# Two attention layers on one core: a per-batch schedule, looped over the batches, replaced by one written-out list over all sixteen units

## The reference, cut to what matters

```python
# layer 0                                     # layer 1
q, k, v = split(xn @ Wqkv.T)                  kc = conv(xn, Wconv, stride=3); k_tmp = cat(xn[:, :1], kc)
scores = q @ k.T / sqrt(8)                    q = xn @ Wq.T; k = k_tmp @ Wk.T; v = k_tmp @ Wv.T
scores = where(qi >= ki, scores, -inf)        scores = q @ k.T / sqrt(8) - 1e9 * (3*ki >= qi + 0.001)
o = softmax(scores) @ v; x += o @ Wo.T        o = softmax(scores) @ v; x += o @ Wo.T + bo
```

## Time and profile before

| | |
|---|---|
| median of 3 runs | 1368.36 us (1366.69 to 1369.11) |
| profiled execution | 1375.63 us, its span 1373.7 us |
| attention of layer 0 | 246.8 to 766.9 us of the span |
| attention of layer 1 | 886.1 to 1124.9 us |
| mean granted clock of TensorE | 0.903 of full |

### The profile page before, as it was taken

The page is one execution under the profiler, slowest core; times in us unless marked ns, Lnnn a source line. Parts: engine busy times, 40 slices in busy tenths (PEclk is TensorE's granted clock), DMA queues, the critical chain, the costliest instruction groups (busy, mean ns, idle before and its releaser), DMA issues. The chain is left out here.

```text
span 1373.7 us, 25353 instructions
## 1 busy us (share of the span) xinstructions
PE 1147.1 (84%) x7394; PEld 634.9 (46%) x7394; DVE 1012.1 (74%) x2140; ACT 721.2 (52%) x1105; POOL 562.2 (41%) x821
## 2 busy tenths in 40 slices
PE   0665667899989998999999666699999969999984
PEld 0433455334434443444343344444444427888863
DVE  5997999788868886888784254477767627777788
ACT  0552222056656665666567442045656557777772
POOL 5455322013423331333222253346667571565663
PEclk9877898599999999999999787579999889999996
DMA  3333790001221211121100023112222115577542
GB/s 100 93 117 112 115 109 0 3 15 60 89 88 48 71 63 57 48 71 63 40 2 2 1 75 99 40 33 65 57 56 68 33 56 186 168 234 237 178 123 62
DMA packets 98595, 107.75 MB, mean 78 GB/s; under 512 B 16226, under 2 KB 76455, under 8 KB 98481
## 3 DMA queue, kind: packets, MB, share of 16 engines
q1 hardware_dynamic: 93488, 97.83, 26.1%
q0 software_dynamic: 4992, 8.48, 1.8%
HBM read 64.67 MB, written 42.63 MB: 78 GB/s over the span
## 5 line engine op out<-in xcount | busy, mean ns | idle before, releaser
L1105 ACT ACTIVATE a_probs<-a_pst 128x1024 f32<-128x1024 f32 (+4 forms) x544 | 417.9, 812 | 276.5 <-PE a_pst L1035 274.1
L1130 DVE TENSOR_REDUCE a_tops<-a_ps 128x1 f32<-128x512 f32 (+9 forms) x624 | 343.4, 589 | 77.4 <-PE a_ps L1004 73.0
L946 POOL TENSOR_SCALAR_AFFINE_SELECT a_probs<-a_probs 128x256 f32<-128x256 f32 (+3 forms) x384 | 181.7, 482 | 429.5 <-ACT a_probs L1105 426.3
L1004 PE MATMUL a_ps<-kp,qp 96*128 96x512 bf16 (+9 forms) x1280 | 313.4, 314 | 8.6 <-issue 6.6
L1035 PE MATMUL a_pst<-qp,kp 99*128 99x512 bf16 (+4 forms) x1088 | 264.4, 336 | 5.4 <-ACT a_probs L1105 4.6
L1058 PE MATMUL a_po<-a_probs,vh 128*32 128x512 f32 (+4 forms) x2176 | 233.6, 501 | 7.5 <-POOL a_probs L946 6.7
L1130 DVE TENSOR_REDUCE a_tops_lead<-a_ps 128x1 f32<-128x512 f32 x256 | 166.9, 685 | 39.4 <-PE a_ps L1004 36.9
L1004 PEld LDWEIGHTS a_ps<-kp,qp 96*128 96x128 bf16 x1280 | 115.0, 103 | 118.1 <-DVE a_tops_lead L1130 34.0
L1001 PE MATMUL a_ps<-mask_s,identb 128*128 128x128 bf16 (+8 forms) x624 | 148.5, 239 | 12.7 <-DVE a_tops L1130 4.7
L1035 PEld LDWEIGHTS a_pst<-qp,kp 99*128 99x128 bf16 (+1 forms) x1088 | 97.7, 101 | 79.1 <-ACT a_probs L1105 36.9
L1001 PEld LDWEIGHTS a_ps<-mask_s,identb 128*128 128x128 bf16 x624 | 60.1, 99 | 153.8 <-DVE a_tops L1130 90.3
(11 more groups left out here) (262 smaller groups left out, 1800.6 us busy)
## 6 DMA issues: line engine op xcount, KB each, us to landing
e_slot_w<-weight_parts SPq DMA_DIRECT2D x23, 1024.0 KB
weight_parts<-a_cut SPq DMA_DIRECT2D x18, 512.0 KB, 4.2
k_parts<-o SPq DMA_DIRECT2D x48, 128.0 KB
qp<-q_parts SPq DMA_DIRECT2D x64, 96.0 KB
kp<-k_parts SPq DMA_DIRECT2D x32, 192.0 KB
slot_rows<-empty_row SPq DMA_DIRECT2D x4, 1495.0 KB, 26.8
e_slot_x<-slot_rows SPq DMA_DIRECT2D x23, 260.0 KB, 3.6
a_raw<-in_wraw SPq DMA_DIRECT2D x18, 256.0 KB, 4.3
```

The lines of the kernel that those rows point to most:

```text
L946: pool.affine_select(out=seen, in_=seen, compare_op=ALU.is_ge, fill=0.0, base=m0, pattern=[[0, 2], [1, mw]], channel_multiplier=-1 if laye ...
L1004: last = pe.matmul(bank[:, i * room:i * room + w], sb["qp"][slot][0:KROWS, j, f["qt"] * P:(f["qt"] + 1) * P], sb["kp"][slot][0:KROWS, j // ...
L1105: act.activation(probs[local % RING][0:st["rows"], 2 * part:2 * part + 2, st["off"]:CHUNK], p_st[part][0:st["rows"], :, st["off"]:CHUNK], ...
L1130: dve.tensor_reduce(out, scores, AX.X, ALU.max).then_inc(s["banks_read"], 1)
```

## The change

`batch_schedule`, `TUNING`, `batches` and the hardware loop go. `Geometry.order` makes one list for all sixteen units of a layer. It steps through time: it keeps a clock for each of PE, DVE, ACT and POOL, gives each operation a duration from constants at the top of the file, and appends at each step the entry whose inputs are ready first (with a rank where several are ready). The engines' code then has batch and unit numbers that are constants, in both layers. The arithmetic, the tiles, the number of banks (3) and of buffers for probabilities (4) are as before.

```diff
-TUNING = [(13, 2800, 2200), (13, 2500, 2200)]
+COLUMN_US, LOAD_US, PASS_US, LANE_US, REDUCE_US, EXP_US, EXP_COLUMN_US, TAIL_US, STORE_US, LOADED_US = (
+    0.00042, 0.105, 0.07, 0.00104, 0.165, 0.17, 0.00083, 1.1, 2.2, 9.0)
+AHEAD = (0.35, 0.6)
+RING = 4
...
+            if n < units and (k or n in maxima_end) and (n * S + k < RING or n * S + k - RING in sums_end):
+                ready.append((max(pe, score_banks[half] + PASS_US, maxima_end[n]), 3, "pair"))
...
+            m, f = fills // F, fills % F
+            if m < units and m in loaded and m < n + 2 and not (turns and f == F - 1) and (m < 2 or m - 2 in split_end):
+                behind = m + fills_share[f] < at + 1 + AHEAD[self.layer]
+                ready.append((max(bank, loaded[m]), 2 if behind else 5, "fill"))
+            start, _, what = min((r if r[0] > pe + PASS_US else (pe, r[1], r[2])) for r in ready)
...
+            if what == "turn_max":
+                m = turns.pop(0)
+                pe = start + LOAD_US
+                banks[mine] = dve = max(dve, pe + PASS_US) + REDUCE_US
+                maxima_end[m] = dve + STORE_US
+                order.append(("turn_max", m, 0, 0))
...
+                if k == S - 1 and half and n + GROUPS < units:
+                    order.append(("next_load", n, 0, 0))
+                    loaded[n + GROUPS] = pe + LOADED_US
...
-        def batches(eng, body):
-
-            if layer == 0:
-                with eng.Fori(0, B - 1) as b:
-                    body(b, geo.batch_schedule(False, False), False)
-            else:
-                for b in range(B - 1):
-                    body(b, geo.batch_schedule(False, False), False)
-            body(B - 1, geo.batch_schedule(False, True), True)
...
+            for what, n, k, part in order:
...
+                if what == "turn_max":
+                    sp.wait_ge(s["banks_read"], read(use))
+
+                    sp.dma_start(sb["qp"][n % GROUPS][KROWS:KROWS + PARTS, :, :].rearrange("r j t -> r (j t)"),
+                                 top_rows[:, :]).then_inc(s["maxima_stored"], 16)
+                if what == "next_load":
+                    sp.wait_ge(s["scores_t_ready"], since["scores_t_ready"] + 2 * S * (n + 1))
+                    load_operands(sp, sb, dram, layer, geo.keys, n // GROUPS + 1, n % GROUPS)
```

More of the change, by code:

```diff
@@ L713, in __init__ @@
         self.split = 5 if layer == 0 else 4
[L717 to L799, removed]
@@ L806, in counted_before @@
     ends = T // CHUNK * units
-    uses = geo.uses_before(B - 1, False) + geo.last_uses
+    uses = sum(what in BANK_USES for what, *_ in geo.order())
     layer0 = dict(banks_filled=uses, banks_read=uses, split_steps=units * geo.split, maxima_stored=16 * units, scores_t_ready=2 * units * geo.S,
@@ L844, in attention, with filled, read @@
         block = ctx.enter_context(nc.Block())
[L846 to L852, removed]
+        order = geo.order()
+        def filled(use):
+            return since["banks_filled"] + use + 1
+        def read(use):
+            return since["banks_read"] + use + 1
         def raw_load(sp, b, i):
             sp.wait_ge(e["cut_done"], START + 2 * (BATCH_CUTS * b + max(0, i - 1)))
-            sp.dma_start(raw[i % 2][:, :], io["wraw"][bass.ds(b * BATCH_CUTS + i, 1), :, :].rearrange("c p h -> (c p) h"))\
+            sp.dma_start(raw[i % 2][:, :], io["wraw"][b * BATCH_CUTS + i, :, :])\
                 .then_inc(sb["raw_in"][i % 2], 16)
@@ L1056, in weigh @@
                 for j in range(GH):
-                    last = pe.matmul(p_o[VW * j:VW * (j + 1), c0:c1], sb["vh"][g % 2][0:st["rows"], st["kt"], j, :],
-                                     probs[local % RING][0:st["rows"], j, c0:c1],
-                                     start=st["first"] and half == 0, stop=st["last"], tile_position=(0, VW * j),
+                    last = pe.matmul(p_o[VW * j:VW * (j + 1), st["off"]:CHUNK], sb["vh"][n % 2][0:st["rows"], st["kt"], j, :],
+                                     probs[local % RING][0:st["rows"], j, st["off"]:CHUNK],
+                                     start=st["first"], stop=st["last"], tile_position=(0, VW * j),
@@ L1061, in weigh @@
                                      skip_group_check=True)
-                if half == len(halves) - 1:
-                    last.then_inc(s["pv_done"], 1)
-            def run(b, schedule, last):
-                use = 0
-                for what, g, k, part in schedule:
-                    if what == "fill":
-                        fill(b, g, k, use)
-                    if what == "pair":
-                        pair(b, g, k, part, g * S + k)
-                    if what == "weigh":
-                        weigh(b, g, k, part, g * S + k)
-                    if what == "turn_max":
-                        turn_max(b, b * GROUPS + g, use)
-                    if what == "turn_out":
-                        turn_out(b, b * GROUPS + g, k, use)
-                    use += what in BANK_USES
@@ L1080, in first @@
-            def first(schedule):
-                for use, (what, g, k, part) in enumerate(x for x in schedule if x[0] in BANK_USES):
-                    if what == "fill":
-                        fill(0, g, k, use, first=True)
-                    if what == "turn_max":
-                        turn_max(0, 0, use, first=True)
-            first(geo.batch_schedule(True, False))
-            batches(pe, run)
+                last.then_inc(s["pv_done"], 1)
+            use = 0
+            for what, n, k, part in order:
+                if what == "fill":
+                    fill(n, k, use)
+                if what == "pair":
+                    pair(n, k, part)
+                if what == "weigh":
+                    weigh(n, k)
+                if what == "turn_max":
+                    turn_max(n, use)
+                if what == "turn_out":
+                    turn_out(n, k, use)
+                use += what in BANK_USES
@@ L1115, in _ @@
-            batches(act, run)
+            use, last_out = 0, None
+            for what, n, k, part in order:
+                if what == "turn_out":
+                    last_out = use
+                use += what in BANK_USES
+                if what == "pair":
+                    st, local = geo.steps[k], n * S + k
+                    if part == 0 and local >= RING:
+                        act.wait_ge(s["pv_done"], since["pv_done"] + local - RING + 1)
+                    act.wait_ge(s["scores_t_ready"], since["scores_t_ready"] + 2 * local + part + 1)
+                    act.activation(probs[local % RING][0:st["rows"], 2 * part:2 * part + 2, st["off"]:CHUNK],
+                                   p_st[part][0:st["rows"], :, st["off"]:CHUNK], ACT.Exp)\
+                        .then_inc(s["exp_done"], 1)
+                if what == "end":
+                    act.wait_ge(s["pv_done"], since["pv_done"] + S * n + 1 + max(
+                        i for i, st in enumerate(geo.steps) if st["c"] == k))
+                    if last_out is not None:
+                        act.wait_ge(s["banks_filled"], filled(last_out))
+                    act.activation(o_raw[:, :], p_o[:, :], ACT.Copy).then_inc(s["o_copied"], 1)
@@ L1170, in scale_out @@
                     .then_inc(s["banks_read"], 1)
-            def run(b, schedule, last, first=False):
-                use = 0
-                for what, g, k, part in schedule:
-                    if what == "fill":
-                        fill(b, g, k, use, first)
-                    if what == "tail":
-                        tail(b, g, use, first)
-                    if what == "turn_max":
-                        copy_max(b, b * GROUPS + g, use, first)
-                    if what == "turn_out":
-                        scale_out(b, g, k, use)
-                    use += what in BANK_USES
-            run(0, geo.batch_schedule(True, False), True, first=True)
-            batches(dve, run)
+            use = 0
+            for what, n, k, part in order:
+                if what == "fill":
+                    fill(n, k, use)
+                if what == "tail":
+                    tail(n, use)
+                if what == "turn_max":
+                    copy_max(n, use)
+                if what == "turn_out":
+                    scale_out(n, k, use)
+                use += what in BANK_USES
 def store_q1(sp, sb, dram, b, c):
```

272 lines of the change are left out of this document (148 added, 124 removed).

## The result

| | before | after | forecast of after |
|---|---|---|---|
| median of 7 runs, us | 1368.36 | 1381.52 | 1361.7 (1340 to 1378) |
| profiled execution, us | 1375.63 | 1383.19 | 1368.9 |
| attention of layer 0, us | 520.5 | 542.0 | 529.4 |
| attention of layer 1, us | 239.0 | 223.7 | 223.4 |

The changed kernel is 0.9% slower: ratio 1.0087, interval 1.0066 to 1.0108. It is also above the forecast's range. The stage between the layers (118.8 us both times) and what follows layer 1 (248.5 and 248.4) did not move. The start of layer 0 is 1.9 us later.

A forecast was written before the change was run, and what follows sets the result against it. PE was taken as the bound, with waits at batch boundaries. Layer 0's +8.9 and layer 1's −15.6 gave −6.7 us: profiled 1375.6 to 1368.9, median 1368.4 to 1361.7 us, range 1340 to 1378.

The forecast's parts named there:

- 4, standing for the store: Layer 0, units 2, 3, 5, 7, 9, 11: PE waits for the store behind eight loads, +22.6 us (19 to 27).
- 5, clock behind the stalls: Layer 0: a slower clock after five stalls, 1.85 us each, +9.3 us (0 to 25).
- 1, boundaries: Layer 0, batch boundaries: the list runs through them without a loop end, −15.5 us.
- 3, inside units: Layer 0, inside 14 units: half of the 0.9 us of removable waiting goes, −6.5 us (0 to −12.6).
- 2, first and last unit: Layer 0, first and last unit: a small gain from the new order, −1 us (0 to −5).
- Rival C: Layer 0, slower clock after five stalls: +25 us instead of +9.3, total 1377 us; chance 0.20.
- A: Whole kernel, the forecast itself: 1361.7 us, its own range 1354 to 1369; chance 0.50.
- Rival B: Layer 0: the store does not wait behind the loads, so no stalls or slow clock, 1330 us; chance 0.13.
- Rival D: Both layers, inside units: the waits stay and nothing is gained, +12 us, 1374 us; chance 0.17.
- Layer 1: Layer 1's attention: boundaries −12.1, first and last unit −1.5, inside units −2; −15.6 us in all.

The follow-up runs named there:

- e4: Changed kernel with extra matmuls that nobody reads run on PE while it waits for the store in six units of layer 0; 1366.83 us.
- e1: Changed kernel with SP issuing the store of the maxima ahead of the eight loads of next_load in six units of layer 0; 1338.45 us.
- e6: Kernel of e1 with the store priced at 3.2 us instead of 2.2 in layer 1's list; 1335.68 us.
- e3: Kernel before, its own order kept, with layer 0's three batches written out instead of a hardware loop; 1359.75 us.
- e7: As e1, but in the six units four of the eight loads stay ahead of the store and four go behind; 1350.27 us.
- e9: Kernel before, unchanged, profiled a second time; 1372.5 us.
- e8: Kernel of e1 with the store priced at 3.2 us in layer 0's list and 4.0 us in layer 1's; 1348.73 us.
- e2: Changed kernel with the store of the maxima issued by ScalarE's queue, the loads staying on SP's; 1345.16 us.
- e5: Changed kernel with the list's price of the store in layer 0 set to 8.0 us instead of 2.2; 1358.41 us.
- e10: Changed kernel, unchanged, profiled a second time; 1383.7 us.

## Why the forecast was wrong

The forecast found the mechanism and its six places and gave it too small a price; nothing that it did not name decided. In layer 0, from the readings above:

| part | forecast | measured | from |
|---|---|---|---|
| 4, standing for the store | +22.6 | +26.9 | the six waits (e4 − e1 26.1, e4 − e6 28.1) |
| 5, clock behind the stalls | +9.3 | +13.8 | after − e4 |
| 1, boundaries | −15.5 | −15.5 | before to e3 −10.3; then three times 31.8 − 30.07 |
| 3, inside units | −6.5 | −5.6 | 14 times 29.68 − 30.08 |
| 2, first and last unit | −1 | +1.9 | what is left |
| sum | +8.9 | +21.5 | |

**The step that failed in part 4 is the landing of the store.** The forecast let data move up to 2.0 us behind the store's begin and took 0.1 more to the pair. Data that have moved are not yet a pair that runs: with no load ahead it is 2.6 to 2.8 us from the store's begin to the pair in nearly all units of both layers, and behind the eight loads 2.80, 2.80, 2.94, 3.01, 3.24 and 3.34. The mean of the five long stalls is 4.7 us, not 4.1, and unit 2's is 3.27, not 2.1. The other terms of the stall held: the eight issues took 5.75 us against 5.8 in all units but unit 3 (6.21), and PE's cover was 4.14 us against 4.0. The upper bound, 27, had come from longer loads; it held the 26.9 for another reason.

**The step that failed in part 5 is the price of the clock**, and it missed by as much. It took 1.85 us a stall from loop ends of 3.2 and 3.4 us of standing, and it counted five stalls. The clock fell behind all six, at 2.3 each in the mean. Why a stall costs 1.6 us in one unit and 3.1 in another stays open; its length does not tell it (e4). Rival C was the right direction with the wrong size: it decided from 3.2 a stall, with 5 as its price. The truth lay between A and C, and it was enough because two terms were short together.

**The other missed terms** are smaller. Part 2 left out that the last unit's store has less work ahead of it: 1.45 us of standing at 764.83, and 0.3 ahead of the first pair of unit 0. How parts 2 and 3 share their sum is an allotment: in every kernel that keeps this list in layer 0 the interval from unit 1 to unit 2 is 33.1 us, while the stretch behind the last copy is some 2 us shorter than before. Their sum, −3.7 against −7.5, is firm to some 2 us. Rival B fell with e7: the store waits for issues in proportion. Rival D fell in layer 0, where e1 shows 0.4 us gained in a unit, and held in layer 1.

**Layer 1** came out at −15.4 against −15.6, but by luck in its parts. Of the 239.0 us before, 3.4 were that one execution's clock (e9). Inside the units 13.1 us replaced some 12.7: a loss of about 6 us in 15 intervals where −2 was forecast, nearly all of it 14 waits of 0.4 us for the store, again from the 2.7 us to the pair. The boundaries of e9 are 3.9 to 4.6 above an ordinary unit rather than 3.1, which paid for a part.

**From the profile to the median** the forecast took 7.2 us off, as before has it. After has its profile only 1.7 above its median. That adds 5.6 us, and it is chance: e1's profile, with its slow stretch, is 4.4 above its median. Layer 0's 12.6, the later start's 1.9, layer 1's 0.2 and small change are the rest of the 19.8 us between 1361.7 and 1381.5. Why the attention begins at 248.1 to 249.0 in some of these kernels (after, e1, e4, e7, e8) and at 246.3 to 247.2 in others (before, e2, e3, e5, e6) was not tried; e1 and e6 differ in layer 1's order alone.

**What the Trainium skill says** of issuing time, "DMA: Bandwidth & Descriptors", section Issuing engines are not separate DMA queues, that it is usually small relative to the DMA itself: here one issue takes 0.6 to 0.8 us against the 2.7 of the store as a whole, a quarter, so the forecast said too much with "disagrees". What the sentence does not tell is the sum: eight issues held SP for 5.74 us, twice the store's 2.7, and e7 shows the wait falling with their number. The sum by rival B was 1330; the kernel whose stalls are gone measured 1338.

## What to carry to other kernels

A list that orders TensorE by stepping through time should step through every queue that its entries touch: this one priced the store and not the eight load issues ahead of it, and that was the difference between 1381.5 and 1338.5 us. No run here has a list with a clock for SP; e5, with one crude price for it, got 1358.4. Where a small gain is forecast as the difference of large terms (here −39 and +32), it stands or falls with the worst-known term; time a wait to the instruction that it releases, not to the data's last movement. And where an urgent small transfer shares a queue with a bulk of patient ones, try first to let it pass: it was a change of one queue's order and left every other engine's order as it was.

## What the runs showed of the hardware

The five stalls of TensorE of 1.5 to 2.1 us in e7 left the granted clock at full speed; behind one of 1.59 us in e1 it fell, behind one of 1.46 in e6 it did not. Stalls of 4.4 to 5.1 us, and unit 2's of 3.27, were each followed by rows at 1.2 GHz, in both profiles of the changed kernel, and the six together cost 13.8 us beyond the standing. Matmuls that nobody reads, run in the stall, gave these back (e4): 1381.5 to 1366.8 us.

A store of 96 rows takes 2.6 to 2.8 us from the begin of its issue to the matmul that it releases, where no load is near. Directly behind eight loads on the same queue it took 2.8 to 3.34 us, or 3.5 in the second profile (e10). Issued on another queue while eight loads were being issued (e2) it took 2.68 to 2.94 us in five units, but 3.81 and 3.60 in two others.
